# Two layers of attention and experts on one core: 128-row operands in the second layer, later copy of merged tokens and inputs ahead of weights in the routing

## The reference, cut to what matters

```
x  = L0_attn_x                                  # (8, 512, 256)
xn = layernorm(x)
x  = x + attention(xn) + routed_experts(xn)     # first layer
xn = layernorm(x)
x  = x + memory(xn) + block_ffn(xn)             # second layer

routed_experts:  logits = xn @ gate_w.T + gate_b        # 32 experts
                 probs  = softmax over the tokens; each expert takes its best 8 tokens
                 merged = sum of these tokens, weighted; h = gelu(merged @ w1 + b1)
                 o = h @ w2 + b2, given back to the 8 tokens with the same weights
memory:          gelu((xn @ W_K.T) @ W1.T) @ W2.T        # 64 hidden columns
block_ffn:       prob = softmax(xn @ router_w.T + router_b)   # 16 blocks of 64
                 h = relu(xn @ w1.T + b1), kept only in the 4 best blocks of a token
                 y = h @ w2.T + b2
```

## Time and profile before

| | |
|---|---|
| median of 3 timed runs | 1491.17 us (1486.17 to 1493.72) |
| the profiled execution | 1487.67 us, its span 1485.9 us |
| TensorE matmuls | 1414.3 us busy, 95% of the span |
| weight loads | 1089.7 us |
| VectorE | 990.7 us, 67% |
| ScalarE | 914.2 us, 62% |
| GpSimd | 165.5 us, 11% |
| mean granted TensorE clock | 0.973 of full speed |
| bytes moved | 122.90 MB, 83 GB/s in the mean |

### The profile page before, as it was taken

How to read it: one execution, slowest core, us unless ns; L and a number is a source line. 1 busy time by engine, 2 the same in 40 slices (tenths; PEclk the granted TensorE clock), 3 DMA queues, 4 the chain that set the end, 5 groups by cost and what they waited for, 6 DMA issues and landing times.

```text
span 1485.9 us, 28161 instructions
## 1 busy us (share of the span) xinstructions
PE 1414.3 (95%) x9680; PEld 1089.7 (73%) x9680; DVE 990.7 (67%) x3164; ACT 914.2 (62%) x2292; POOL 165.5 (11%) x559
## 2 busy tenths in 40 slices
PE   3779999999999999999999999999998899999998
PEld 2566778777877877777777778777775778878787
DVE  5837885888587678757876885878587544444442
ACT  4637785878588577848866784877577433333332
POOL 4501110111011101101110110111011000000000
PEclk9779999999999999999999999999999999999999
DMA  5542322232223222323231322222230311111100
GB/s 202 193 161 79 99 94 80 80 121 71 93 67 108 83 85 76 114 67 102 96 98 61 99 94 80 80 97 84 75 94 6 87 39 40 40 39 40 39 15 29
DMA packets 88303, 122.90 MB, mean 83 GB/s; under 512 B 8561, under 2 KB 74466, under 8 KB 88162
## 3 DMA queue, kind: packets, MB, share of 16 engines
q1 hardware_dynamic: 85554, 116.35, 24.4%
q10 hardware_dynamic: 2608, 4.76, 0.9%
HBM read 101.69 MB, written 19.40 MB: 81 GB/s over the span
## 4 chain that ended last, share of the span: by engine, by line
PE 88%; ACT 4%; DVE 1%; issue 1%; DMA 0%; SPq 0%; ACTq 0%; DVEq 0%
PE at L797 18%; PE at L806 11%; PE at L882 10%; PE at L1467 8%; PE at L857 8%; PE at L923 7%; PE at L1503 6%; PE at L811 3%; PE at L892 2%; PE at L909 2%; PE at L849 2%; PE at L837 2%; PE at L1486 2%; PE at L842 2%; ACT L1063 1%; ACT probT L1054 1%
## 5 line engine op out<-in xcount | busy, mean ns | idle before, releaser
L1045 ACT ACTIVATE prob<-prob,low 128x512 f32<-128x512 f32 (+3 forms) x512 | 280.6, 550 | 70.5 <-DVE low L1178 70.5
L1178 DVE CUSTOM_DVE_ANT_0 prob<-at,mask 128x512 f32<-128x512 f32 (+3 forms) x512 | 220.4, 486 | 78.7 <-PE at L811 78.7
L1054 ACT ACTIVATE probT<-at 128x512 f32<-128x512 f32 (+1 forms) x256 | 131.5, 540 | 123.1 <-PE at L857 123.0
L806 PE MATMUL at<-kT,qT 64*128 64x512 f32 (+3 forms) x1024 | 194.0, 460 | 8.8 <-DVE up_lo L1231 5.0
L797 PE MATMUL at<-w_hi,cT_lo 128*128 128x386 f32 x512 | 197.3, 385 | 5.1 <-DVE area_raw L1127 4.3
L797 PE MATMUL at<-w_hi,cT_hi 128*128 128x386 f32 x512 | 174.8, 342 | 0.0
L797 PE MATMUL at<-w_lo,cT_hi 128*128 128x386 f32 x512 | 174.7, 341 | 0.0
L857 PEld LDWEIGHTS at<-ident,prob 128*128 128x128 f32 x1280 | 142.4, 141 | 40.0 <-issue 36.8
L857 PE MATMUL at<-ident,prob 128*128 128x128 f32 x1280 | 164.4, 275 | 2.1 <-DVE prob L1191 1.9
L1191 DVE TENSOR_SCALAR prob<-prob,rec 128x512 f32<-128x512 f32 (+3 forms) x512 | 163.3, 383 | 4.5
L882 PE MATMUL at<-probT,v 128*64 128x512 f32 (+3 forms) x1024 | 152.8, 440 | 0.1
(11 more groups left out here) (216 smaller groups left out, 2563.4 us busy)
## 6 DMA issues: line engine op xcount, KB each, us to landing
area_w<-in_L_ffn_w SPq DMA_DIRECT2D x64, 1024.0 KB, 5.6
bias<-in_L_ffn_w SPq DMA_DIRECT2D x160, 32.0 KB, 3.7
x_in<-in_L_attn_x SPq DMA_DIRECT2D x8, 512.0 KB, 5.8
xr<-in_L_attn_x SPq DMA_DIRECT2D x8, 512.0 KB, 4.0
eo_d<-eo SPq DMA_DIRECT2D x32, 128.0 KB, 1.8
x_d<-xr SPq DMA_DIRECT2D x8, 512.0 KB, 2.9
area_raw<-x_d SPq DMA_DIRECT2D x8, 512.0 KB, 4.0
out<-area_raw SPq DMA_DIRECT2D x8, 512.0 KB, 2.9
```

Of the source, the lines that this page charges most:

```text
L806: eng.matmul(bS[i][:, at:at + (c + 1) * P], qT[rows, c * P:(c + 1) * P], kT[rows, 0:(c + 1) * P], start=True, stop=False)
L1045: eng.activation(sl, sl, ACT.Exp, scale=-1.0, bias=low[:, i:i + 1], accum_out=den[:, i:i + 1]).then_inc(exp_done.sem, 1)
L1054: eng.activation(probT[h][:, x:y], bR[i][:, 0:y - x], ACT.Copy).then_inc(done.sem, 1)
L1178: eng.tensor_tensor_reduce(out=prob[s % 2][h][:, off[c]:off[c + 1]], in0=bS[i][:, at:at + (c + 1) * P], in1=mask[:, (NT - 1 - c) * P:T], s ...
```

## The change

It makes `spread`, `sp`, `shutT`, `mem` and `backT` tiles of 128 partitions. The rows that were not there before are filled with zeros by POOL: `backT` in the routing, `shutT` before `sp` at the end of the attention, rows 64 to 127 of `mem` ahead of its row of ones. In the routing, TensorE does `gate(0)` before `turn_x(1)`; ACT does `copy_merged(b-1)` after `exp(b)`, instead of `copy_merged(b)` at the end of a round; and u, the keys' weights, omega, Wq, Wk, Wv and Wproj are issued by SP behind the three inputs, instead of by ACT.

```
-         ("sp", [NB, HC, P], F32), ("spread", [NB, HC, P], F32R), ("shutT", [NB, 2, T], F32R),
+         ("sp", [P, HC, P], F32), ("spread", [P, HC, P], F32R), ("shutT", [P, 2, T], F32R),
-        backT=sb("backT", [M1 + 1, C]),
+        backT=sb("backT", [P, C]),
...
                 get(1)
                 get(2)
+                for dst, src in ((u_in[:, :, :], t["L0_attn_u"].partition_broadcast(P)),
+                                 (kw[:, :], t["L0_attn_k_rms_w"].partition_broadcast(P)),
+                                 (om[:, :], t["L0_attn_omega"].partition_broadcast(P))):
+                    eng.dma_start(dst, src).then_inc(u_load.sem, 16)
+                for i, name in enumerate(("L0_attn_Wq", "L0_attn_Wk", "L0_attn_Wv")):
+                    eng.dma_start(raw_w[:, :, i, :], t[name].rearrange("(k p) n -> p k n", p=P)).then_inc(w_load.sem, 16)
...
+                eng.dma_start(w_proj[:, :, :], t["L0_attn_Wproj"].rearrange("(h p) c -> p h c", p=P)).then_inc(wp_load.sem, 16)
                 for b in range(B):
                     put(b)
...
                 turn_x(0)
+                gate(0)
                 turn_x(1)
-                gate(0)
...
                     exp(b)
+                    if b > 0:
+                        copy_merged(b - 1)
                     if b + 2 < B:
                         norm(b + 2)
...
                     copy_pick(b)
-                    copy_merged(b)
+                copy_merged(B - 1)
...
-                for tile in (tok[:, :, :], bias2[:, :], ag[:, :, :].bitcast(F32), kaug[:, :].bitcast(F32)):
+                for tile in (tok[:, :, :], bias2[:, :], ag[:, :, :].bitcast(F32), kaug[:, :].bitcast(F32), g["backT"][:, :]):
                     eng.memset(tile, 0.0)
...
-            (("hT_hi", [P, HC, T], F32R), ("hT_lo", [P, HC, T], F32R), ("mem", [M1 + 1, T], F32)))
+            (("hT_hi", [P, HC, T], F32R), ("hT_lo", [P, HC, T], F32R), ("mem", [P, T], F32)))
...
+                eng.memset(shutT[:, :, :].bitcast(F32), 0.0).then_inc(spread_set.sem, 1)
                 eng.memset(sp[:, :, :], 1.0).then_inc(spread_set.sem, 1)
...
     def gpsimd(eng):
+        eng.memset(mem[M1:P, :], 0.0).then_inc(mem_one.sem, mem_one.unit)
+        eng.wait_ge(mem_one.sem, mem_one.at(0, 1))
         eng.memset(mem[M1:M1 + 1, :], 1.0).then_inc(mem_one.sem, mem_one.unit)
...
-            eng.tensor_copy(shutT[:, b % 2, :], bF[0][0:NB, :]).then_inc(shutT_done.sem, shutT_done.unit)
+            eng.tensor_copy(shutT[0:NB, b % 2, :], bF[0][0:NB, :]).then_inc(shutT_done.sem, shutT_done.unit)
```

More of the change, by code:

```diff
@@ L331, in _ @@
             def _(eng):
[L332 to L337, removed]
                 for rows in (slice(0, D), slice(D, P)):
@@ L340, in _ @@
                         eng.dma_start(qk_w[rows, i:i + 1], t[name].unsqueeze(1)).then_inc(qk_load.sem, 16)
-                eng.dma_start(w_proj[:, :, :], t["L0_attn_Wproj"].rearrange("(h p) c -> p h c", p=P)).then_inc(wp_load.sem, 16)
                 eng.preload_act_table_set("natural_log_exp_and_others")
@@ L666, in attend @@
         pe_prep = ev("pe_prep", 1)
-        prep_hi, prep_done, spread_set, prepared = ev("prep_hi", 1), ev("prep_done", 1), ev("spread_set", 4), ev("prepared", 1)
+        prep_hi, prep_done, spread_set, prepared = ev("prep_hi", 1), ev("prep_done", 1), ev("spread_set", 5), ev("prepared", 1)
         def begins_in(s):
@@ L1331, in _ @@
                          allow_small_or_imprecise_dtypes=True).then_inc(spread_set.sem, 1)
+                eng.memset(shutT[:, :, :].bitcast(F32), 0.0).then_inc(spread_set.sem, 1)
                 eng.memset(sp[:, :, :], 1.0).then_inc(spread_set.sem, 1)
-                eng.wait_ge(spread_set.sem, spread_set.at(0, 2))
+                eng.wait_ge(spread_set.sem, spread_set.at(0, 3))
                 width = HC * P // NB
@@ L1336, in _ @@
                                   pattern=[[P, HC], [1, P]], channel_multiplier=-width).then_inc(spread_set.sem, 1)
-                eng.wait_ge(spread_set.sem, spread_set.at(0, 3))
+                eng.wait_ge(spread_set.sem, spread_set.at(0, 4))
                 eng.affine_select(out=sp[:, :, :], in_=sp[:, :, :], compare_op=ALU.is_ge, fill=0.0,
@@ L1340, in _ @@
                 eng.wait_ge(pe_p1.sem, pe_p1.at(NTURN - 1))
+                eng.wait_ge(spread_set.sem, spread_set.at(0))
                 second.gpsimd(eng)
@@ L1394, in second_layer @@
         ev("logit_done", 1), ev("route", 2 * NT + 3), ev("shut_done", 1), ev("shutT_done", 1), ev("out_done", 2))
-    rstd_done, mem_one = ev("rstd_done", 1), ev("mem_one", 1)
+    rstd_done, mem_one = ev("rstd_done", 1), ev("mem_one", 2)
     def get_x(eng, b):
```

## The result

The changed kernel took 1444.45 us (median of 4 runs, 1443.79 to 1444.74), the kernel before beside it 1488.99 us (4 runs, 1486.17 to 1493.72). The ratio is 0.9697 with a 95% interval of 0.9668 to 0.9726, so 44.5 us less. The profiled execution took 1444.28 us with a span of 1442.5 us.

What follows compares the result with a forecast made beforehand. TensorE was taken to bound most of the kernel, DVE and the order of waits the routing. 1487.7 - 24.4 + 1.0 - 11.9 - 14.0 = 1438.4 us, plus 1.8 to the median, gave 1440.2 us, range 1431 to 1457.

Steps and rivals of the forecast that it cites:

- Part 1: Second layer, 16-row matmul of `up`: 128 rows remove its pauses, about 24.4 us, less 1.0 us of waits for ACT.
- rival (c): Second layer: 128-row weight loads lie open, so padding gains nothing and only the routing gains; 1477.2 us, chance 0.04.
- The rule quoted for that rival: On TensorE, weight loads overlap with matmuls in flight only when their row group differs; so padding would gain nothing.
- The sum: Whole kernel, profiled execution: 1487.7 - 24.4 + 1.0 - 11.9 - 14.0 = 1438.4 us.
- Part 2: Second layer, matmul of `mem` and `backT` with 128 rows instead of 65: gains nothing, bounds 0 and -2 us.
- Part 3: Second layer: four half-clock stretches behind routers go, since less idle time tips the clock; 11.9 us.
- rival (a): Second layer: the half-clock stretches stay because the routers they follow stay as they are; 1452.1 us, chance 0.28.
- Part 4: Start of the routing: earlier inputs and the moved gate(0) bring the first top-8 to 19.5 from 26.16, 6.6 us.
- the last step of that part: Routing's input queue: 4.6 MB of weights and the inputs are through by about 19 us, before input 3's moments at 23.
- Rival (b): Routing: only the start gains, because DVE waits behind weights and stores or is full; 9.3 more, 1449.5 us, chance 0.10.
- Part 5: Routing rounds: moving ACT's `copy_merged` gains 1.0 us in the first three, 5.0 in the next four, 1.4 in the last.
- The 1.0 us of the first three rounds: Routing, first to fourth top-8: 24.2 us, with DVE busy for 23.0 as the bound, would shorten by 1.0 us.

Runs made afterwards that it cites:

- the mirror runs: Changed kernel with 16 rows again in the first matmul of `up`, in chunks 0 to 5 or only in chunks 6 and 7: 1461.67 and 1459.29 us.

## Why the prediction was right, and where it was not

1440.2 us were predicted with a range of 1431 to 1457, and 1444.45 came.

**Part 1, the pauses.** Right in mechanism and about in size. The rival (c) fell with the load at 1189.17, which starts beside a matmul of the same 128 rows, as the one at 1199.52 had in the kernel before.
The rule quoted for that rival from the Trainium skill (TensorE: Matmul & The Clock Gate, The mechanism) does not hold in this trace.

Pauses and clock can be told apart batch by batch. From the first chunk of a batch to that of the next (the last one: to the last matmul) the kernel before took 38.34, 35.26, 35.27, 38.33, 36.77, 38.35, 33.54 and 28.91 us, the changed one 32.29, 32.28, 32.29, 32.30, 32.31, 32.30, 30.57 and 25.98. The second batch, before and after, has no half-clock stretch in either:

```profile
1235.10:1270.36 35.26, 35.26 (x203) 28.59 (x203) 16.50 (x46) 11.69 (x19) 1.01 (x1) 1.00 0.14 41
```

```profile
1220.08:1252.36 32.28, 32.28 (x204) 28.88 (x203) 16.42 (x46) 11.71 (x19) 1.01 (x1) 1.00 0.16 45
```

A batch gains 2.98 us at full clock, the last two 2.97 and 2.93, which makes 23.8 us with ACT's waits already taken off. The run with 64 rows, all its pauses at full clock, says 24.1. The sum had 23.7 - 1.0 = 22.7 at full clock. ACT's ReLU makes a chunk 0.03 us longer where it is waited for, 20 times, so about 0.6 us instead of 1.0, and in as many chunks as were counted for it.

**Part 2, 65 rows.** Right: no gain. The run with 65 rows in the other matmul agrees: 65 rows cost no pause there either.

**Part 3, the clock.** That all four stretches go was right, their price was not quite. The four batches that had one are longer than 35.27 us by 3.07, 3.06, 1.50 and 3.08 us: 10.7 for 23.9 us of half clock, 0.45 a microsecond and not 0.5. The sum had 11.9 here and, in part 1, another 0.7 for the pauses in these stretches, which the 11.9 already contained. The reason given, idle time beside the router, was only near it. The place was right (the mirror runs), the pause was not the cause (64 rows), so it was in part luck that the change, which took out both the pauses and the few rows, removed the stretches. The rival (a), at 1452.1, fell: the stretches did go.

**Part 4, the start.** 6.9 us for 6.6. What failed is the last step of that part: "at the 401 GB/s [...] they and the inputs are through by about 19 us". That rate was taken for the whole time from the first issue on, but it held only from 14 us. All transfers in one queue moved 2.4 MB until then, and input 3 behind them was not there before 27.4 us. The step named its own check (DVE waits for input 3) and it went against it. Rival (b) was right in its cause and too large in its price: the routing fell short of the sum by 4.8 us, not 9.3. That no price was put on a late input 3 ("if it came late, DVE would wait for it") is the step that cost most.

**Part 5, the rounds.** The last two stages came as worked out, -5.2 for -5.0 and -1.4 for -1.4, and at like clocks the move of the copy is worth 4.7 to 5.1 and 1.4 us. The 1.0 us of the first three rounds failed: the second to the fourth top-8 took 17.11 us before and after. The prediction had named the reason itself, DVE is the bound there; waits taken off ACT give nothing while DVE is busy.

**From the execution to the median.** Half of the 3.5 us between profile and median was added; after the change that difference is 0.2. This gave back 1.6 us of the miss. Together: 1438.4 was summed for the execution and 1444.3 came, 5.9 more, of which 5.3 are the second stage (4.3 lost and 1.0 not gained), 0.8 the second layer and 0.4 the attention, less 0.3 at the start, 0.2 in the later rounds and 0.1 ahead of the first chunk.

## What to carry to other kernels

Where a matmul with few rows stands between full ones, look at its weight load: if it starts only with its own matmul, and its neighbours lie further apart than the rest, try filling its operands with zero rows: here, from 16 or 64 rows to 128, it cost one memset an operand and took the pause away on both sides. When transfers are put in one queue in the order in which they are wanted, the next input behind the weights is part of that order; work out when it is wanted, and take the rate from the stretch in which these bytes really move. Moving one engine's wait gives something only in rounds where the other engines have idle time: here nothing in the first three rounds, where DVE was full, and about 5 us in the next four.

## What the hardware showed that was not expected

The border lies between 64 and 65 rows, and at 64 rows it costs as much as at 16: a second layer of 274.44 us against 250.80.

The half clock went with the number of rows that work behind a stretch of 16-column matmuls: 16 rows gave it behind 10 of 21 routers, 64 rows, with the same pauses, behind none of 14. Its price was 10.7 us for 23.9 us of it, less than the half.

The routing's length goes with the clock that its execution is granted: with the same instructions it ended between 78.91 and 85.11 us. From the fourth to the eighth top-8 it took 23.5 us at a clock of 1.00, 24.5 at 0.73 and 27.4 at 0.64. A gain of 2 us there can't be read from one execution without that number beside it.
